# High and low part of a head's queries in one stationary tile

## What is computed

```python
q = x @ Wq
k = context @ Wk
v = context @ Wv
...
sim = jnp.einsum('bhid,bhjd->bhij', q, k) * SCALE
attn = jax.nn.softmax(sim, axis=-1)
out = jnp.einsum('bhij,bhjd->bhid', attn, v)
...
return out @ Wo + bo
```

## Time and profile before

| | before |
|---|---|
| median of 3 runs | 596.3 us |
| span of the profiled execution | 602.2 us |
| PE busy | 522.3 us, 87% |
| PE weight loads busy | 476.4 us, 79% |
| DVE busy | 340.4 us, 57% |
| ACT busy | 282.2 us, 47% |
| POOL busy | 231.9 us, 39% |
| first score matmul | 32.09 us |
| last score matmul | 319.1 us |

### The profile page before, as it was taken

The page is one execution under the profiler, slowest core; times in us unless marked ns, Lnnn a source line. Parts: engine busy times, 40 slices in busy tenths (PEclk is TensorE's granted clock), DMA queues, the critical chain, the costliest instruction groups (busy, mean ns, idle before and its releaser), DMA issues.

```text
span 602.2 us, 12363 instructions
## 1 busy us (share of the span) xinstructions
PE 522.3 (87%) x3712; PEld 476.4 (79%) x3713; DVE 340.4 (57%) x783; ACT 282.2 (47%) x866; POOL 231.9 (39%) x319
## 2 busy tenths in 40 slices
PE   8999999999999999998998420699988998999991
PEld 6789999998989889898998410588877877888881
DVE  5856666677586585765756764255444544533330
ACT  3446556555465555564553112355543544533330
POOL 5160000337008780077704625043433433443333
PEclk9999999999999999999999755799999999999995
DMA  8500000001000100001010995636446436333322
GB/s 246 181 2 1 0 2 2 20 1 35 3 0 26 44 20 15 0 10 63 2 36 1 224 229 178 206 84 151 109 90 156 117 76 157 53 51 53 55 36 26
DMA packets 32372, 41.54 MB, mean 69 GB/s; under 512 B 3088, under 2 KB 28432, under 8 KB 32336
## 3 DMA queue, kind: packets, MB, share of 16 engines
q1 hardware_dynamic: 25184, 31.75, 17.9%
q0 software_dynamic: 7152, 9.33, 9.9%
HBM read 24.12 MB, written 16.95 MB: 68 GB/s over the span
## 4 chain that ended last, share of the span: by engine, by line
PE 34%; issue 26%; DVE 11%; ACT 8%; DMA 6%; POOL 6%; POOLq 3%; DVEq 2%; SPq 2%; another core or an unknown queue 1%; ACTq 0%
PE bank L603 7%; PE bank L581 6%; ACT probs L773 5%; PE bank L527 4%; POOL tok L1225 4%; PE bank L543 4%; PE bank L1279 3%; PE bank L557 3%; DMA expert_queue<-zrow 3%; DVE nmax L892 2%; POOLq L1233 2%; DMA out_dram<-yq,to_row 2%; PE bank L706 2%; PE bank L501 2%; DVEq L902 1%
## 5 line engine op out<-in xcount | busy, mean ns | idle before, releaser
L773 ACT ACTIVATE probs<-bank,nmax 128x154 f32<-128x154 f32 x256 | 97.6, 388 | 123.6 <-DVE nmax L892 119.3
L581 PE MATMUL bank<-vdiag,pT 128*128 128x128 f32 (+2 forms) x640 | 80.0, 272 | 7.1 <-DVE oT_lo L916 6.9
L581 PEld LDWEIGHTS bank<-vdiag,pT 128*128 128x128 f32 (+1 forms) x640 | 77.5, 191 | 10.5 <-DVE oT_lo L916 10.3
L1234 POOL DMA_INDIRECT out_dram<-yq,to_row x39 | 61.8, 1585 | 33.7 <-issue 24.1
L1279 PE MATMUL bank<-gu_hi,xqT_hi 128*128 x156 | 68.7, 441 | 1.1 <-DVE xqT_lo L1396 1.1
L892 DVE TENSOR_REDUCE nmax<-bank 128x2 f32<-128x308 f32 x128 | 60.1, 471 | 7.7 <-PE bank L543 6.8
L1279 PE MATMUL bank<-gu_hi,xqT_lo 128*128 x156 | 61.9, 397 | 0.0
L1279 PE MATMUL bank<-gu_lo,xqT_hi 128*128 x156 | 61.7, 396 | 0.0
L1408 DVE TENSOR_TENSOR hidT_lo<-bank,hidT_hi 128x512 fp32r<-128x512 f32 x39 | 26.9, 690 | 53.1 <-ACT hidT_hi L1355 53.1
L1403 DVE TENSOR_TENSOR hid<-hid,bank 128x512 f32<-128x512 f32 x39 | 26.8, 688 | 52.6 <-PE bank L1279 52.6
L557 PE MATMUL bank<-ident,probs 128*128 128x128 f32 (+1 forms) x320 | 46.2, 273 | 5.6 <-ACT xfT L786 2.9
(11 more groups left out here) (183 smaller groups left out, 1432.4 us busy)
## 6 DMA issues: line engine op xcount, KB each, us to landing
gu_raw<-in_gate_up_wT_dram SPq DMA_DIRECT2D x8, 1024.0 KB, 5.0
expert_queue<-zrow SPq DMA_DIRECT2D x8, 642.5 KB
xq<-expert_queue SPq DMA_DIRECT2D x39, 128.5 KB, 2.5
dn_raw<-in_down_wT_dram SPq DMA_DIRECT2D x8, 512.0 KB, 6.0
x<-in_x_dram SPq DMA_DIRECT2D x4, 512.0 KB, 13.0
out_dram<-out SPq DMA_DIRECT2D x8, 256.0 KB, 2.2
wq_raw<-in_L_xattn_Wq_dram SPq DMA_DIRECT2D x1, 1024.0 KB, 11.5
wo_raw<-in_L_xattn_Wo_dram SPq DMA_DIRECT2D x1, 1024.0 KB, 10.6
```

The lines of the kernel that those rows point to most:

```text
L581: last = nc.tensor.matmul(at[:, col0 + j0 * DH:col0 + j0 * DH + n], pT[u % 2][0:rows, b, :], v, start=(b == 0), stop=(b == NBLK - 1), skip ...
L773: last = nc.scalar.activation(probs[u % 4][:, j * NKB:(j + 1) * NKB], S_BANK[hf][:, m * NKB:(m + 1) * NKB], ACT.Exp, bias=nmax[:, u % 4, j ...
L1234: nc.gpsimd.indirect_dma_start(out[:, :], bass.IndirectOffsetOnAxis(to_row[:, 0:1], 0), yq[p % 2][:, :], None, compute_op=ALU.add).then_in ...
```

## The change

The query tiles `q_hi` and `q_lo` become one tile, `q_parts`, with 128 partitions for each single head ("side" of the pair): the high part of the head's 64 queries on the head's own 64 partitions, the low part on the other 64. `k_hi` holds for each side the high part of the head's keys twice, on both halves of the partitions; `k_lo` holds the low part on the head's own half and zeros on the other. One matmul of `q_parts` with `k_hi` then sums high times high and low times high; a second one with `k_lo` adds high times low. Each has 154 columns, and there are two per head, four per pair.

```diff
-            k_hi = asb("k_hi", [P, H // 2, B, 2 * NKB], F32R)
-            k_lo = asb("k_lo", [P, H // 2, B, 2 * NKB], F32R)
+            k_hi = asb("k_hi", [P, H // 2, 2, B, NKB], F32R)
+            k_lo = asb("k_lo", [P, H // 2, 2, B, NKB], F32R)
...
-                q_hi[n] = asb(f"q_hi{n}", [P, H // 2, GT], F32R)
-                q_lo[n] = asb(f"q_lo{n}", [P, H // 2, GT], F32R)
+                q_parts[n] = asb(f"q_parts{n}", [P, H // 2, 2, GT], F32R)
...
+            HALVES = (slice(0, DH), slice(DH, P))
...
-                        n = 0
-                        for q, k in ((q_hi, k_hi), (q_hi, k_lo), (q_lo, k_hi)):
-                            last = nc.tensor.matmul(S_BANK[hf][:, 0:2 * NKB], q[par][:, pair, tok:tok + P], k[:, pair, par, :],
-                                                    start=(n == 0), stop=(n == 2))
-                            n += 1
+                        for side in range(2):
+                            for k in (k_hi, k_lo):
+                                last = nc.tensor.matmul(S_BANK[hf][:, side * NKB:(side + 1) * NKB], q_parts[par][:, pair, side, tok:tok + P],
+                                                        k[:, pair, side, par, :], start=(k is k_hi), stop=(k is k_lo))
...
-                    for a in range(2):
-                        half = slice(a * DH, (a + 1) * DH)
-                        last = nc.scalar.activation(k_hi[half, m, :, a * NKB:(a + 1) * NKB],
-                                                    bank[m % 4][half, 0:B * NKB].rearrange("p (b k) -> p b k", b=B), ACT.Copy, scale=SCALE)
+                    for side, half in enumerate(HALVES):
+                        for to in HALVES:
+                            last = nc.scalar.activation(k_hi[to, m, side, :, :].rearrange("p b k -> p (b k)"), bank[m % 4][half, 0:B * NKB],
+                                                        ACT.Copy, scale=SCALE)
...
-                        last = nc.scalar.copy(q_hi[par][:, 2 * k - 2:2 * k, :].rearrange("p m t -> p (m t)"), at[:, :])
+                        for side, half in enumerate(HALVES):
+                            last = nc.scalar.copy(q_parts[par][half, 2 * k - 2:2 * k, side, :], at[half, :].rearrange("p (m t) -> p m t", m=2))
...
-                for half, keys in zero_keys:
-                    last = nc.vector.memset(k_hi[half, :, :, keys].bitcast(F32), 0.0)
-                last.then_inc(s["k_zero"], 1)
...
-                        last = nc.vector.tensor_tensor(q_lo[par][:, queries, :].rearrange("p m t -> p (m t)"), at[:, :],
-                                                       q_hi[par][:, queries, :].rearrange("p m t -> p (m t)").bitcast(F32), ALU.subtract)
+                        for side, half in enumerate(HALVES):
+                            last = nc.vector.tensor_tensor(q_parts[par][HALVES[1 - side], queries, side, :], at[half, :].rearrange("p (m t) -> p m t", m=2),
+                                                           q_parts[par][half, queries, side, :].bitcast(F32), ALU.subtract)
```

More of the change, by code:

```diff
@@ L198, in gated_xattn_moe @@
                 wq_raw = early.enter_context(nc.sbuf_tensor("wq_raw", [P, KD, INNER], F32))
-            q_hi, q_lo = [None, None], [None, None]
+            q_parts = [None, None]
             for n in (1, 0):
-                q_hi[n] = asb(f"q_hi{n}", [P, H // 2, GT], F32R)
-                q_lo[n] = asb(f"q_lo{n}", [P, H // 2, GT], F32R)
+                q_parts[n] = asb(f"q_parts{n}", [P, H // 2, 2, GT], F32R)
             before = asb("before", [P, P], BF16)
@@ L268, in two_tiles @@
                 return x1[:, first:first + 2, :] if isinstance(i, int) else x1[:, bass.ds(first, 2), :]
-            zero_keys = ((slice(DH, P), slice(0, NKB)), (slice(0, DH), slice(NKB, 2 * NKB)))
+            HALVES = (slice(0, DH), slice(DH, P))
             @block.sync
@@ L353, in _ @@
                 nc.gpsimd.drain()
-                for half, keys in zero_keys:
-                    nc.gpsimd.memset(k_lo[half, :, :, keys].bitcast(F32), 0.0).then_inc(s["k_zero"], 1)
+                for side in range(2):
+                    nc.gpsimd.memset(k_lo[HALVES[1 - side], :, side, :, :].rearrange("p m b k -> p m (b k)").bitcast(F32), 0.0).then_inc(s["k_zero"], 1)
                     nc.gpsimd.drain()
@@ L722, in _ @@
                     first_job(k)
-                pe.wait_ge(s["k_zero"], 3)
+                pe.wait_ge(s["k_zero"], 2)
                 for u in range(2):
@@ L1084, in _ @@
                     dve.wait_ge(s["k_hi"], m + 1)
[L1085 to L1088, removed]
+                    for side, half in enumerate(HALVES):
+                        last = nc.vector.scalar_tensor_tensor(k_lo[half, m, side, :, :].rearrange("p b k -> p (b k)"), bank[m % 4][half, 0:B * NKB], SCALE,
+                                                              k_hi[half, m, side, :, :].rearrange("p b k -> p (b k)").bitcast(F32), ALU.mult, ALU.subtract)
                     last.then_inc(s["k_lo"], 1)
```

## The result

The changed kernel takes **654.88 us** (median of 4 runs, 652.82 to 655.96), the kernel before beside it 597.89 us. The ratio is 1.093, 95% interval 1.089 to 1.097. Run again beside other kernels, it took 650.26 us against 597.01, ratio 1.091 (1.086 to 1.096). Slower was right; 630 us and the range to 650 were too low. It cost 53 to 57 us where I had 33. Executions more than 1.5% above the fastest of their kernel are left out of the ratios; that concerns experiment 1 alone, whose profiled execution is one of two such.

What follows compares the result with a forecast made beforehand. A ring through ACT, DVE and PE, closed by a single PSUM bank, was taken to bound slots 4 to 6. Loop 29.4, last slots 0.4 and before the loop 3.4, added to 596.3, gave 630 us, range 612 to 650.

Steps and rivals of the forecast that it cites:

- the sum: Whole kernel: 29.4 us in the loop, 0.4 in the last eight slots, 3.4 before the loop, added to the 596.3 us median.
- more idle time on PE: Sign expected in the profile after: PE idles longer ahead of the scores and of the product of L581; no size given.
- The ring: Query casts (ACT) and low parts (DVE) in series: +2.6 us in slots 4-7, +1.2 in slot 3 after 0.13 slack.
- together 4.2 us per group: Eight attention slots: 2.6 us in slots 4 to 7, 1.2 in slot 3, 0.4 of score matmuls; seven groups make 29.4.
- the score matmuls' term: PE in attention: four short matmuls at 0.112 us replace three, +0.025 us per half unit, 0.4 per eight slots, 3.2 in all.
- The price of a half: Query parts on ACT and DVE: 64 partitions cost as much as 128, adding 0.60 and 0.71 us, 1.31 us per job.
- float32 streaming: Rival for the score matmuls: 154 columns stream no faster than plain float32, 0.26 us each; 673 us, chance 0.13.
- half price: Rival for query parts and keys: 64 partitions take less or the halves overlap; +5 to +12, 605 us, chance 0.08.
- the free load: Rival for score matmuls: a repeated stationary tile loads free, PE gains 18 us; 582 us if parts are hidden, chance 0.04.
- the jobs' term: Before the loop: the third query job waits for the bank of the first, whose parts end later; +1.2 us.
- The keys: Before the loop: four ACT activations per pair of heads take 1.73 us and set the pace; +2.2 us.
- a rival on the matmuls: Score matmuls of 0.2 us, between the forecast's own price and plain float32's: 650 us, chance 0.05.

Runs made afterwards that it cites:

- experiment 1: Kernel before, with only the high and low part of each query job made by two 64-partition instructions instead of one: 636.56 us, ratio 1.068.
- experiment 6: Changed kernel, with DVE making the low part of a query job one slot later, behind the second maxima: 608.18 us, ratio 1.023.
- experiment 7: Kernel before, with both query parts split into two instructions and the low part one slot later on DVE: 596.11 us, ratio 0.999.
- experiment 5: Kernel before, with only the high part of each query job split into two 64-partition instructions: 611.04 us, ratio 1.025.
- experiment 2: Changed kernel with its four score matmuls, but each query part made by one 128-partition instruction: 605.81 us, ratio 1.016.
- experiment 3: Kernel before, with four key activations per pair of heads instead of two: 599.62 us, ratio 1.008.
- experiment 8: Changed kernel, with 45 matmuls added on PE between the keys' projection and the first input's transposes: 649.82 us, ratio 1.091.
- experiment 4: Changed kernel, with 22 matmuls added on PE at the head of each slot 7 with output projection and earlier job: 646.46 us, again 647.39.

## Why the prediction was wrong

- **The step that failed** is the sum, in "I add them to the median": it priced all of PE's work behind a wait at the duration that it has in rows with a clock of 1.00. The forecast named "more idle time on PE" as a sign to look for and gave it no price. What the runs showed in its place is that the granted clock fell during such idle time or soon behind it. That cost 13.3 us in the seven slots 7 (58.2 against 44.9), 1.7 in one slot 2 with routing work, 1.4 in one slot 4 and 1.7 before the loop, 18 us in all. The rest of the loop's growth, 32 us, came at full clock. With 6.3 us before the loop, its 1.7 of the clock among them, this makes 55 us; 53 and 57 were measured.
- **The ring** was right in place and nearly in size. Experiments 1, 6 and 7 show that most of the loss is the order on DVE and not the amount of work, and experiment 5 that its slack was read rightly. But that "together 4.2 us per group" met 4.3 is in part luck: 0.4 of it was the score matmuls' term. The ring itself costs 4.3 where 3.8 were worked out, since slots 2 and 5 grew by 0.4 each, which the sum did not have. The groups with routing work and the first group deviate too, and seven groups make 32 us in place of 29.4.
- **The price of a half** was right, 0.58 and 0.69 us.
- **The score matmuls** were priced too high: four take 0.41 us where 0.448 were worked out and three of 308 columns take 0.43, so the term of 3.2 us is about nothing (experiment 2). Still, the rivals on float32 streaming, on half price and on the free load are out: the distances are 0.11 us, also from the third to the fourth, which have the same stationary tile.
- **Before the loop**, the jobs' term was right, 1.3 for 1.2. The keys, for which 2.2 were worked out, cost 1.9 in experiment 3, 2.8 in the changed kernel and 2.4 in experiment 8.
- That the clock is the cause in slot 7 is shown by experiment 4's profiles, in which the slot is 6.41 us again with slot 6 as long as it was. How much time a kernel without any fall would win in all is open: the added matmuls held the clock in five of seven groups, and the total moved by less than its interval. The top of the range, 650, had been set by a rival on the matmuls, and no case held a price for the clock.

## What to carry to other kernels

Look in the chain of waits for instructions of the helping engines that stand in series between two uses of a single PSUM bank; whatever is added there counts in full, however idle those engines look on average. Here two instructions of half the partitions cost twice one of all: don't lay operands out so that a copy must be made by halves, or first move that copy behind what the next round waits for. When an edit makes PE wait, price the work behind the wait at the lower clock too, above all if its longest block follows. And when a total agrees with the forecast, read it group by group: 2.9 us that looked like a term of 3.2 were something else.

## What the runs showed of the hardware

- In the changed kernel a wait of PE of 2.1 us (1.55 in two groups) stood ahead of each of seven slots 7, and in each the granted clock went to 1.2 GHz for a part; 256-column matmuls then start 0.22 us apart in place of 0.12. The length of the wait alone does not decide it. In experiment 1's profile the clock fell behind four of seven such waits, and of two waits of 2.6 us in the changed kernel it fell at one. In experiment 5's profile, with waits of up to 1.8 us, it did not fall in the loop; in experiment 6's it fell three times, with no wait above 1.1 us near.
- Successive instructions of 64 partitions on different halves don't overlap: 0.01 us lies between the end of the one and the start of the next, on ACT and DVE, and each takes as long as one of 128 partitions.
- A matmul of 154 columns with its load of 128 costs 0.11 us in a stream, also when the stationary tile is the same as before; the first of a block is followed after 0.07 to 0.08 us where a projection runs ahead of it and after 0.15 where transposes do. A block of four takes 0.41 or 0.49 us accordingly, one of three of 308 columns 0.43 or 0.51.
